# Moving value, query and key units between the slots of an attention-plus-experts kernel

## The reference

```
q, k = low-rank projections of xn: (xn @ a[h]) @ b[h], 16 heads, rank 64, head width 16
v    = xn @ v_w.T + v_b
att  = softmax(causal(q k^T / 4));  y = att v;  attn = y @ o_w.T + o_b
ffn  : probs = softmax(xn @ choice_w.T), 8 experts; each takes its top 128 tokens of a batch,
       silu(x_in @ w1) @ w2, times the gate, added to the token's row
out  = x + attn + ffn
```

## Time and profile before

| | |
|---|---|
| median of 3 runs | 1301.05 us |
| the profiled execution | 1295.71 us, span 1293.8 us |
| TensorE (PE) busy | 1184.1 us, 92% |
| VectorE (DVE) busy | 967.2 us, 75% |
| ScalarE (ACT) busy | 668.7 us, 52% |
| GpSimd (POOL) busy | 692.0 us, 53% |
| mean granted TensorE clock | 0.969 of full speed |

### The profile page before, as it was taken

How to read it: one execution, slowest core, us unless ns; L and a number is a source line. 1 busy time by engine, 2 the same in 40 slices (tenths; PEclk the granted TensorE clock), 3 DMA queues, 4 the chain that set the end, 5 groups by cost and what they waited for, 6 DMA issues and landing times. The chain is left out here.

```text
span 1293.8 us, 29459 instructions
## 1 busy us (share of the span) xinstructions
PE 1184.1 (92%) x8502; PEld 819.8 (63%) x8502; DVE 967.2 (75%) x3293; ACT 668.7 (52%) x1312; POOL 692.0 (53%) x1021
## 2 busy tenths in 40 slices
PE   6799999999999999999999998769999999999995
PEld 5545555555555555555555553348988888888885
DVE  3588888879889888888888879935666666666662
ACT  2357667667667677677667665522332323233320
POOL 1235344355355355345345443344888888888885
PEclk9779999999999999999999999979999999999998
DMA  5443443443443443443444342132555555556454
GB/s 141 114 116 83 116 116 100 116 116 98 115 115 98 115 115 99 115 115 100 113 115 112 100 99 67 34 114 38 111 99 95 114 93 102 94 100 109 85 78 53
DMA packets 106287, 130.31 MB, mean 101 GB/s; under 512 B 21580, under 2 KB 75476, under 8 KB 106196
## 3 DMA queue, kind: packets, MB, share of 16 engines
q1 hardware_dynamic: 76356, 94.46, 28.1%
q0 software_dynamic: 24576, 33.57, 15.6%
q10 hardware_dynamic: 5264, 1.32, 0.5%
HBM read 44.84 MB, written 33.55 MB: 61 GB/s over the span
## 5 line engine op out<-in xcount | busy, mean ns | idle before, releaser
L719 DVE CUSTOM_DVE_ANT_0 junk<-bank,rowmask 128x256 bf16<-128x256 f32 (+3 forms) x1024 | 454.9, 485 | 60.3 <-PE bank L866 38.0
L565 ACT ACTIVATE probs<-bank 128x512 f32<-128x512 f32 x640 | 377.3, 598 | 158.0 <-PE bank L887 143.8
L469 POOL TENSOR_SCALAR_AFFINE_SELECT probs<-probs 128x256 f32<-128x256 f32 (+1 forms) x640 | 224.2, 363 | 311.0 <-ACT probs L565 308.9
L866 PE MATMUL bank<-kstk,qstk 96*128 96x256 bf16 (+3 forms) x1024 | 250.7, 306 | 34.3 <-DVE rowmax L719 17.3
L887 PE MATMUL bank<-qstk,kstk 98*128 98x256 bf16 (+3 forms) x1024 | 251.0, 307 | 3.8 <-ACT probs L565 2.6
L1049 POOL DMA_INDIRECT out_rows<-mixed,rows x128 | 208.9, 1632 | 58.2 <-issue 38.1
L1078 ACT ACTIVATE hid<-bank 128x512 f32<-128x512 f32 x128 | 76.6, 598 | 228.5 <-PE bank L1141 228.5
L908 PE MATMUL bank<-probs,vaug 128*32 128x512 f32 (+3 forms) x2048 | 168.5, 448 | 6.6 <-POOL probs L469 6.6
L1157 PE MATMUL bank<-w_hi,hid_hi 128*128 128x256 f32 x512 | 147.3, 288 | 0.0
L1157 PE MATMUL bank<-w_hi,hid_lo 128*128 128x256 f32 x512 | 144.9, 283 | 0.0
L1157 PE MATMUL bank<-w_lo,hid_hi 128*128 128x256 f32 x512 | 144.8, 283 | 0.0
(11 more groups left out here) (131 smaller groups left out, 2097.8 us busy)
## 6 DMA issues: line engine op xcount, KB each, us to landing
qstk<-qk_part SPq DMA_DIRECT2D x96, 256.0 KB, 4.8
kstk<-qk_part SPq DMA_DIRECT2D x96, 256.0 KB, 4.7
xln<-in_L_attn_hidden_states SPq DMA_DIRECT2D x16, 512.0 KB, 6.1
xn_rows<-xn SPq DMA_DIRECT2D x16, 512.0 KB, 2.8
xres<-in_L_attn_hidden_states SPq DMA_DIRECT2D x16, 512.0 KB, 3.6
out_rows<-xres SPq DMA_DIRECT2D x16, 512.0 KB, 2.9
qstk<-in_L_ffn_w SPq DMA_DIRECT2D x8, 512.0 KB, 4.0
kstk<-in_L_ffn_w SPq DMA_DIRECT2D x8, 512.0 KB, 3.9
```

The lines of the kernel that those rows point to most:

```text
L469: nc.gpsimd.affine_select(out=block, in_=block, compare_op=ALU.is_ge, fill=0.0, base=0, pattern=[[0, len(cols)], [1, P]], channel_multipli ...
L565: nc.scalar.activation(probs[n % 2][:, 512 * k:512 * k + 512], SCORET[k % 2][:], ACT.Exp, scale=SCALE).then_inc(exp_done, 1)
L719: last = nc.vector.tensor_tensor_reduce(out=junk[k % 2][:, col:col + width], in0=SCORE[score_bank(UN * n + k)][:, col:col + width], in1=ro ...
L866: last = nc.tensor.matmul(SCORE[score_bank(UN * n + k)][:, col:col + width], qstk[b % 2][0:KS, GH * g + h, P * i:P * i + P], kstk[b % 2][0 ...
```

## The change

Only the table PROJECTIONS is changed. In slot 0 the value unit at t = 0 goes, and units 0, 1 and 2 stand at t = 8, 9 and 9; unit 3 stays at t = 0 of slot 1. Query unit 0 has its first half at t = 8 of slot 2 and its second at t = 0 of slot 3, followed there by query unit 1 as a whole; their `mid` steps stand at t = 2 and 3. Key unit 2 has its halves at t = 6 and 8 of slot 3, and unit 3 stands whole at t = 9, behind `mid` 2. `mid` 3 stays at t = 1 of the next slot 0.

```diff
 PROJECTIONS = (
-    [(0, "v", 1, 0), (1, "mid", 1, 3), (1, "yt", -1, 0), (2, "xload", 2, 0), (6, "yt", -1, 1), (8, "v", 1, 1),
-     (9, "lnstat", 2, 0), (9, "v", 1, 2)],
-    [(0, "v", 1, 3), (1, "lnstat", 2, 1), (2, "o", -1, 0), (5, "lnapply", 2, 0), (5, "o", -1, 1), (6, "o", -1, 2),
-     (8, "o", -1, 3)],
-    [(0, "xt", 2, 0), (1, "xres", 0, 0), (1, "xt", 2, 1), (6, "qk_first", 2, 0), (8, "qk", 2, 0),
-     (9, "qk_first", 2, 1)],
-    [(0, "qk", 2, 1), (0, "mid", 2, 0), (1, "mid", 2, 1), (4, "qk_first", 2, 2), (6, "qk", 2, 2), (8, "mid", 2, 2),
-     (8, "qk_first", 2, 3), (9, "qk", 2, 3)])
+    [(1, "mid", 1, 3), (1, "yt", -1, 0), (2, "xload", 2, 0), (6, "yt", -1, 1), (8, "v", 1, 0), (9, "lnstat", 2, 0), (9, "v", 1, 1), (9, "v", 1, 2)],
+    [(0, "v", 1, 3), (1, "lnstat", 2, 1), (2, "o", -1, 0), (5, "lnapply", 2, 0), (5, "o", -1, 1), (6, "o", -1, 2), (8, "o", -1, 3)],
+    [(0, "xt", 2, 0), (1, "xres", 0, 0), (1, "xt", 2, 1), (8, "qk_first", 2, 0)],
+    [(0, "qk", 2, 0), (0, "qk_first", 2, 1), (0, "qk", 2, 1), (2, "mid", 2, 0), (3, "mid", 2, 1), (6, "qk_first", 2, 2), (8, "qk", 2, 2), (9, "mid", 2, 2), (9, "qk_first", 2, 3), (9, "qk", 2, 3)])
```

## The result

| | before | after |
|---|---|---|
| median of 4 runs each | 1297.94 us | 1312.28 us |
| range of the runs | 1293.46 to 1301.11 | 1310.51 to 1314.25 |
| ratio, with its 95% interval | | 1.0113 [1.0072, 1.0155] |
| the profiled execution | 1295.71 us | 1314.25 us, span 1312.4 |
| mean granted TensorE clock | 0.969 | 0.960 |

The forecast was 1291.0, within 1280 to 1304, with 0.58 on faster. The time is outside the range and on the other side of before.

The account below looks back on a forecast made before the run. Each batch was bound by the loop through the key stack's transfer, 47.84 us. 13 x 0.75 = 9.75, with 0.25 for the last stack 10.0 us, took the profiled 1295.71 to 1285.7; median forecast 1291.0, range 1280 to 1304.

Parts of the forecast that it names:

- I follow one batch, at the times of 383 to 431 us, and take it times 13.: Attention part: one batch's gain of 0.75 us was taken for 13 batches, 9.75 us in all.
- The clock: TensorE's clock was read as at its upper level, 2.4 GHz, but for two places; no term.
- Chain to the key stack: From last key unit through its split to the key stack's issue: 0.75 us sooner a batch, bounds 0 and 1.3.
- two third-unit steps now next to each other: Steps of key units 2 and 3 on ScalarE and GpSimd might eat the whole gain: lower bound 0.
- Unit 3's first half: Slot 3: the 0.58 us wait before it should go; the last key unit ends 0.25 us sooner.
- Query stack, "Cost 0": Its issue moves from 411.08 to about 412.7 us, still ahead of the key stack's first bytes: cost 0.
- Value units, "the cover holds by 1.0 us": End of slot 0: TensorE ends near 429.0 and the key stack lands last, near 430.3; wait about 1.0 us.
- Rival (c): Slot 3: VectorE runs dry of score products and delays the key stack, 0.6 us a batch, 1309 us; chance 0.16.
- The named signs of failure: Period of 47.8 us or more, VectorE idle over 1 us in slot 3, or row-maxima waits much over 55.6 us.

Follow-up runs that it names:

- e5: The kernel after with the two query roundings one unit earlier, so the query stack is sent earlier: 1307.14 us, ratio 1.0091.
- e12: The kernel before with only the query and key units moved, and both query roundings one unit earlier than in the change: 1292.98 us, ratio 0.9994.
- e1: The kernel before with only slot 0's value units moved as in the change: 1293.01 us against 1293.96 of before, ratio 1.0000.
- e9: The kernel before with VectorE's loop body shifted so that its turn falls between slots 0 and 1: ratio 1.0200.
- e11: The kernel before with only the value units moved, and VectorE's loop turn shifted to between slots 0 and 1: ratio 1.0119.
- e2: The kernel before with only the query and key units and their roundings moved, value units as before: 1302.65 us, ratio 1.0079.
- e8: The kernel after with the rounding of key unit 2 moved to t = 0 of the next slot: 1314.15 us, ratio 1.0143.
- e18: Query and key part of the change on before, query roundings one unit earlier, value unit 0 at t = 2 of slot 0: 1298.98 us, ratio 1.0033.
- e6: The kernel before with two spare 256 KB transfers right behind each query stack, no engine's order changed: 1309.85 us, ratio 1.0119.

## Why the prediction was wrong

- **"I follow one batch, at the times of 383 to 431 us, and take it times 13."** This is the step that failed. The batch I followed has no turn. With one, the kernel before was just covered (TensorE idle 0.62 us, period 47.80 all the same). VectorE's 2.97 us stood in the trace of before; I had looked for who made TensorE wait, and there it hardly shows. In the batches without a turn the sign was right.
- **The clock.** I named the clock as at its upper level and gave it no term. It is the largest: 15.3 us of 19.2.
- **Chain to the key stack, 0.75 us a batch.** Mis-sized, even without a turn: 0.28, the period's 47.81 less 47.53. Of the 0.75, 0.25 was an earlier last key unit and 0.5 a tighter chain behind it. The chain lost 0.17 instead: it took 4.63 us after 4.46, as the negation blocked behind GpSimd put VectorE 0.98 us late. The rest of the loop gained 0.28 + 0.17 = 0.45. The lower bound of this step, "two third-unit steps now next to each other", named the right neighbours and not the mechanism.
- **Unit 3's first half.** Its wait of 0.58 is gone, as forecast. Two sums there don't add up: 0.23 + 0.09 - 0.1 is 0.22 and not 0.25, and 0.41 + 0.23 + 6 x 0.23 is 2.02 and leaves out a product (nine are 0.32 + 8 x 0.23 = 2.16, which is the "about 2.1"). Neither changes the forecast.
- **Query stack, "Cost 0".** Issued 430.43 - 421.39 = 9.04 us ahead of the key stack, at the upper end of the 8 to 9 forecast. But I weighed its place only against the key stack; what it collides with is VectorE's turn. e5 and e12 price that: 1.0 us of turn.
- **Value units, "the cover holds by 1.0 us".** Without a turn it holds by more. The first score product of slot 1 in the kernel after, to set beside the earlier trace rows:

```profile
437.72 0.39 PE L883 MATMUL bank<-qstk,kstk 98*128 98x512 bf16 x1
439.66 0.39 PE L862 MATMUL bank<-kstk,qstk 96*128 96x512 bf16 x1 [1.55 <-DMA kstk<-qk_part]
```

  With a turn it fails: slot 1 starts 392.31 - 378.63 = 13.68 us behind the key-stack issue where 9.23 is the transfer's own, so TensorE, held up and slowed behind the turn, now arrives 4.45 us after the key stack. The value unit at t = 0 was TensorE's work during the turn (e1).
- **Rival (c)** had the right side, and its 1309 is near the 1312 measured, but by luck: it added 8 us where 14 came, and its place is not where the time went, since no score product of slot 3 in the followed batches waits much longer for VectorE (0.4 us in all). The named signs of failure, a period over 47.8 and waits for row maxima much over 55.6 us, are what came. The chance of 0.16 was too low. The sentence of the Trainium skill on interleaving, "Perfetto Trace Analysis", section "Optimization Strategy", would have given the right sign, yet by another way: what mattered of the interleaving was one value unit's place in a stall.

## What to carry to other kernels

Before a batch is taken "times 13", list the periods of all batches and every idle stretch with no releaser: a loop's way back can come once in two batches, and the work beside it is what hides it. When work is moved, ask not only whether the critical transfer still lands last but whether TensorE now stands idle somewhere for longer than before, since its clock may charge that stretch again. Keep large transfers away from the moment at which an engine's loop turns.

## What the runs showed of the hardware

- A turn of VectorE's loop stops that engine for 2.6 to 2.9 us with no transfer under way (e9 to e11). Near the query stack's six transfers it lasted until 11.0 to 11.3 us behind their issue, at the turn near 370 us of before, after, e2, e5, e8 and e12 to e18: 2.95 us where the engine stopped 8.1 us behind it (e5), 4.95 where it stopped 6.2 behind it (e8). Two spare transfers of 256 KB behind them made it 4.14 for 2.97 (e6).
- TensorE's clock fell to 1.2 GHz behind idle stretches of a few us: with 3.25 us at each of five turns a shortfall of 1.7 to 3.4 us every time, with 1.4 to 1.7 us only in some cases (table above), with 0.6 us next to none, and with 12 needless products in the stretch almost none, although VectorE's turn was as long.
- A VectorE instruction of 0.17 us took 1.15 beside GpSimd's subtraction of 1.16.
